# Narrow attentions: projections spread over the loop's first steps, the selection split in halves, the pair mask added in sixteen 32x32 pieces

## The reference

```
q = norm(x) Wq + bq;  k = ctx Wk + bk;  v = ctx Wv + bv
scores[h] = q[h] k[h]^T / sqrt(8)      (+ mask: layer 0 by key, layer 2 by query and key)
out[h]    = softmax(scores[h]) v[h]
layer 2:  of the 128 queries of each head only the 27 with the largest |q[h]|^2 keep their out[h]
x = x + tanh(g) * (out Wo + bo)
```

## Time and profile before

| | us |
|---|---|
| median of 3 runs | 1951.07 (1949.83 to 1951.59) |
| the profiled execution, its own time | 1948.23 |
| its span from the first instruction to the last | 1946.2 |
| TensorE busy | 1779.9 (91% of the span) |
| VectorE busy | 1115.4 (57%) |
| ScalarE busy | 861.5 (44%) |
| GpSimd busy | 613.5 (32%) |

### The profile page before, as it was taken

How to read it: one execution, slowest core, us unless ns; L and a number is a source line. 1 busy time by engine, 2 the same in 40 slices (tenths; PEclk the granted TensorE clock), 3 DMA queues, 4 the chain that set the end, 5 groups by cost and what they waited for, 6 DMA issues and landing times. The chain is left out here.

```text
span 1946.2 us, 43912 instructions
## 1 busy us (share of the span) xinstructions
PE 1779.9 (91%) x16273; PEld 1149.1 (59%) x16273; DVE 1115.4 (57%) x2416; ACT 861.5 (44%) x2151; POOL 613.5 (32%) x1047
## 2 busy tenths in 40 slices
PE   5999878999999999769889999979999989997797
PEld 3555453778778778557763444436777754554343
DVE  4677667566666665561554555552222246776886
ACT  4455425455555555425452333334333344543232
POOL 2667318222222222200103544400000006763440
PEclk9999969999999999869998999978999998999898
DMA  4000040000000000101010000000000010000001
GB/s 108 2 3 3 27 118 6 6 5 7 7 4 7 7 7 2 44 0 44 1 45 1 2 2 2 2 1 0 1 0 0 0 44 2 3 3 2 0 0 43
DMA packets 47708, 27.17 MB, mean 14 GB/s; under 512 B 10928, under 2 KB 44592, under 8 KB 47536
## 3 DMA queue, kind: packets, MB, share of 16 engines
q1 hardware_dynamic: 42800, 24.64, 4.5%
q10 hardware_dynamic: 4736, 0.15, 0.1%
HBM read 22.69 MB, written 2.10 MB: 13 GB/s over the span
## 5 line engine op out<-in xcount | busy, mean ns | idle before, releaser
L708 DVE TENSOR_REDUCE neg_max<-scores 128x8 f32<-128x1024 f32 x192 | 234.8, 1225 | 162.4 <-PE scores L523 66.8
L1708 POOL TENSOR_TENSOR probs<-probs,inverse 128x512 f32<-128x512 f32 x128 | 133.3, 1041 | 337.6 <-DVE inverse L1908 337.6
L651 ACT ACTIVATE probs<-turned 128x1024 f32<-128x1024 f32 x128 | 131.1, 1024 | 224.0 <-PE turned L538 224.0
L493 PE MATMUL scores<-k_diag,q_all 32*128 32x512 f32 x768 | 221.9, 663 | 2.2 <-DVEq L701 2.2
L510 PE MATMUL turned<-q_diag,k_all 32*128 32x512 f32 x768 | 222.0, 653 | 1.1 <-ACT probs L651 1.1
L389 POOL TENSOR_TENSOR k_diag<-k_all,hmask 128x512 f32<-128x512 f32 x96 | 99.8, 1041 | 328.0 <-ACT k_all L630 292.1
L1842 ACT ACTIVATE probs<-scores,neg_max 128x128 f32<-128x128 f32 x512 | 180.7, 387 | 5.3 <-DVE neg_max L1900 5.3
L1409 ACT ACTIVATE hidden_f<-hb_f,b_f 128x512 f32<-128x512 f32 x128 | 88.0, 687 | 130.1 <-PE hb_f L1356 129.9
L1365 PEld LDWEIGHTS yb_f<-w_f,hidden_f 128*128 128x128 f32 x1024 | 119.2, 192 | 14.8 <-issue 14.8
L1365 PE MATMUL yb_f<-w_f,hidden_f 128*128 128x128 f32 x1024 | 119.3, 275 | 0.0
L1356 PE MATMUL hb_f<-xn_all_f,w_f 128*128 (+1 forms) x256 | 118.1, 605 | 0.0
(11 more groups left out here) (292 smaller groups left out, 3675.4 us busy)
## 6 DMA issues: line engine op xcount, KB each, us to landing
ctx_t<-in_ctx_t_dram SPq DMA_DIRECT2D x24, 256.0 KB, 3.2
w_f<-in_L_ffn_W_dram SPq DMA_DIRECT2D x16, 256.0 KB, 3.1
x_state<-in_x_dram SPq DMA_DIRECT2D x4, 512.0 KB, 8.4
ctx_t<-in_ctx_t_dram SPq DMA_DIRECT2D x16, 128.0 KB, 2.1
out_dram<-x_state SPq DMA_DIRECT2D x4, 512.0 KB, 5.4
w_f<-in_L_ffn_We_dram SPq DMA_DIRECT2D x1, 1024.0 KB, 6.8
taps_f<-in_L_ffn_conv_w_dram SPq DMA_DIRECT2D x1, 768.0 KB, 6.4
w_e_f<-_ffn_expert_weights_dram SPq DMA_DIRECT2D x1, 512.0 KB, 4.4
```

The source lines that it names most:

```text
L493: last = nc.tensor.matmul(scores[pair][:, (g % 2) * 512:(g % 2 + 1) * 512], cols(q_all, b, S)[quad_rows(g), :], k_diag[quad_rows(g), b % 2 ...
L651: nc.scalar.activation(probs[:, b % 2, pair, :], turned[:, :], ACT.Exp, **bias).then_inc(s["exp_done"], 1)
L708: v.tensor_reduce(neg_max[:, b % 2, 8 * pair:8 * pair + 8], scores[pair][:, :].rearrange("p (h k) -> p h k", k=S), axis=X_AXIS, op=ALU.max ...
L1708: nc.gpsimd.tensor_tensor(p4, p4, inverse[:, n % 2, CH * h:CH * h + CH].unsqueeze(2).to_broadcast([P, CH, S]), ALU.mult).then_inc(s["prob_ ...
```

## The change

Three things change in the same function.

- **Projections.** `keys_values` is split into `keys` and `values`. Layers 0 and 3 make only two chunks of keys and values and one of queries ahead of the loop (KV0 = 2, TQ0 = 1), layer 2 four chunks of keys and values and all of the queries. The others are made in the loop's first steps: `first_fills` (turned x, keys) at a step's start into `scores[1]`, `second_fills` (queries, values) before `contexts` into `scores[0]`. TensorE waits for the maximum that was last taken from these banks, and each `direct` waits until ScalarE has read the fills. ScalarE reads the first kind before its exponents of the step and the second kind after them. VectorE normalises chunk b+5 within the step in layers 0 and 3; in layer 2 VectorE also copies the turned x, which ScalarE did.
- **Selection.** It gets tiles of its own and works on halves of 16 sequences. The first half is chosen before VectorE's first `maximum`, its ties in the steps -2 and -1; the second half's rounds stand in the steps 1 to 4 and 6, its ties in the steps 8 and 9.
- **Pair mask.** The mask comes laid out by the host in four rotated copies, the last two transposed (128x512 in place of 128x128), and is added by `masks` in 32x32 pieces of the array: eight products of 512 columns for the direct scores and eight for the turned ones, each with another pair of row group and column group.

```diff
-    LATE = 0 if select else 2
+    KV0, TQ0 = (4, NG) if select else (EARLY, 1)
...
-        k_ps, v_ps = turned[:, 0:GW], turned[:, GW:2 * GW]
-        q_ps = [scores[1][:, 0:GW], scores[1][:, GW:2 * GW]]
-        xt_ps = [scores[0][:, 0:GW], heads[1][:, :]]
+        lower, upper = slice(0, GW), slice(GW, 2 * GW)
+
+        def kv_bank(c):
+            if c >= KV0:
+                return scores[1][:, upper], scores[0][:, upper]
+            return (turned[:, lower], turned[:, upper]) if c % 2 == 0 else (heads[0][:, :], heads[1][:, :])
+
+        def tq_bank(c):
+            half = upper if c < TQ0 and c % 2 else lower
+            return scores[1][:, half], scores[0][:, half]
...
+        def first_fills(b):
+
+            return [("t", c) for c in [b + 4] if TQ0 <= c < NG] + [("k", c) for c in [b + 3 + KV0] if KV0 <= c < NG]
+
+        def second_fills(b):
+            return [("q", c) for c in [b + 4] if TQ0 <= c < NG] + [("v", c) for c in [b + 3 + KV0] if KV0 <= c < NG]
...
+            for c in range(EARLY):
+                keys(c)
+                values(c)
+            turn_queries(0)
+            for c in range(TQ0):
...
-            for c in range(EARLY, NG - LATE):
-                keys_values(c)
-            pe.wait_ge(s["q_ready"], NG)
-            pe.wait_ge(s["xnt_done"], NG)
-            if select:
-                topk["tensor"](pe)
+            for c in range(EARLY, KV0):
+                pe.wait_ge(s["k_ready"], c - 1)
+                if c % 2:
+                    topk["norms_read"](pe)
+                keys(c)
+                pe.wait_ge(s["v_ready"], c - 1)
+                values(c)
...
                 if pair == 0:
                     pe.wait_ge(s["kdiag_ready"], b + 1)
+                    pe.wait_ge(s["q_ready"], max(min(b + 1, NG), TQ0))
+                    pe.wait_ge(s["v_ready"], min(b + KV0, NG))
+                    if select:
+                        topk["ranks_read"](pe, b - AHEAD)
+                else:
+                    pe.wait_ge(s["xnt_done"], max(min(b + 2, NG), TQ0))
+                    pe.wait_ge(s["k_ready"], min(b + 1 + KV0, NG))
+                    if select:
+                        topk["ties_read"](pe, b - AHEAD)
...
+            def masks(b_direct, pair, b_cross):
+
+                sides = [(scores[pair], 0, b_direct)] * real(b_direct) + [(turned, 2, b_cross)] * real(b_cross)
+                if mask == "keys" and real(b_direct):
+                    for g in (2 * pair, 2 * pair + 1):
+                        last = nc.tensor.matmul(scores[pair][:, (g % 2) * 512:(g % 2 + 1) * 512], one_row[quad_rows(g), b_direct, :],
                                                 key_rows[quad_rows(g), :].unsqueeze(1).to_broadcast([32, 4, S]),
                                                 start=False, stop=True)
-                    else:
-                        last = nc.tensor.matmul(out, st.identb[:, :], pair_bias[:, :].unsqueeze(1).to_broadcast([P, 4, S]),
-                                                start=False, stop=True)
-                last.then_inc(s_done[pair], 1)
-
-            def crosswise_shift(b, pair):
+                    last.then_inc(s_done[pair], 1)
+                if mask == "pairs":
+                    for out, first, b in sides:
+                        for half in range(2):
+                            for r in range(4):
+                                c = (r + first + half) % 4
+                                last = nc.tensor.matmul(out[quad_rows(c), half * 512:(half + 1) * 512],
+                                                        st.identb[quad_rows(r), quad_rows(r)],
+                                                        pair_bias[quad_rows(r), first + half, :].unsqueeze(1).to_broadcast([32, 4, S]),
+                                                        start=False, stop=first == 0, skip_group_check=True)
+                        if first == 0:
+                            last.then_inc(s_done[pair], 1)
...
-                if mask == "pairs":
-                    for g in (2 * pair, 2 * pair + 1):
-                        nc.tensor.matmul(turned[:, (g % 2) * 512:(g % 2 + 1) * 512], st.identb[:, :],
-                                         pair_turned[:, :].unsqueeze(1).to_broadcast([P, 4, S]), start=False, stop=False)
...
             for b in range(-AHEAD, NB + 1):
+                todo = first_fills(b)
+                if todo or select and b in topk["turn_at"]:
+                    wait(pe, s["max1_done"], b + AHEAD)
+                for kind, c in todo:
+                    fill[kind](c)
+                if select:
+                    topk["turn"](pe, b)
                 direct(b + AHEAD, 0)
                 crosswise(b, 1)
-                direct_mask(b + AHEAD, 0)
-                crosswise_shift(b, 1)
+                masks(b + AHEAD, 0, b)
+                shifts(b, 1)
                 sums(b - 1)
-                if -2 - LATE < b <= -2:
-                    keys_values(NG + b + 1)
                 turn_shift(b + 2)
                 direct(b + AHEAD, 1)
                 crosswise(b + 1, 0)
-                direct_mask(b + AHEAD, 1)
-                crosswise_shift(b + 1, 0)
+                masks(b + AHEAD, 1, b + 1)
+                shifts(b + 1, 0)
+                todo = second_fills(b)
+                if todo or select and b in topk["turn_at"]:
+                    wait(pe, s["max0_done"], b + AHEAD + 1)
+                for kind, c in todo:
+                    fill[kind](c)
+                if select:
+                    topk["rank"](pe, b)
...
             for b in range(-AHEAD, NB):
+                for kind, c in first_fills(b):
+                    read[kind](c)
...
+            normalise(0)
+            dve.wait_ge(loaded, n_loaded)
+            v.tensor_scalar(scaled_bq[:, :], b_q[:, :], scale, None, ALU.mult).then_inc(s["bq_ready"], 1)
             if select:
-                topk["vector"](dve, link)
+                topk["start"](dve)
+            normalise(1)
+            v.tensor_scalar(b_o[:, :], b_o[:, :], gate, None, ALU.mult).then_inc(s["bias_ready"], 1)
             if mask == "keys":
                 dve.wait_ge(s["mask_in"], 80)
-                link(v.tensor_scalar(key_rows[:, :], key_int[:, :], 0, -BIG, ALU.is_equal, ALU.mult))
                 link(v.tensor_scalar(key_cols[:, :], key_int_t[:, :], 0, -BIG, ALU.is_equal, ALU.mult))
-                dve.sem_inc(s["ready"], 1)
-            elif mask == "pairs":
-                dve.wait_ge(s["pair_done"], 1)
-                link(v.tensor_copy(pair_turned[:, :], shift_ps[0][:, 0:S]))
-                dve.sem_inc(s["ready"], 1)
+                v.tensor_scalar(key_rows[:, :], key_int[:, :], 0, -BIG, ALU.is_equal, ALU.mult).then_inc(s["mask_ready"], 1)
+            if select:
+                choose_first, choose_start, choose_middle = topk["vector"](dve)
+                for c in range(NG):
+                    copy_turned(c)
+                    if c + 2 < NG:
+                        normalise(c + 2)
+            if mask == "pairs":
+                dve.wait_ge(s["mask_in"], 16)
+                v.tensor_copy(pair_bias[:, :, :], pair_f[:, :, :]).then_inc(s["mask_ready"], 1)
+            if select:
+                choose_first()
...
+        def ahead_of_loop():
+            read_norms(0)
+            next_eight(0, 0)
+            read_norms(1)
+            for k in range(1, rounds + 1):
+                next_eight(0, k)
+            limits(0)
+
+        def step_start(b):
+            if b in turn_at:
+                ties(turn_at[b])
+            if b - 1 in turn_at:
+                ranks(turn_at[b - 1])
+
+        def step_middle(b):
+            if 1 <= b <= rounds + 1:
+                next_eight(1, b - 1)
+            if b == rounds + 3:
+                limits(1)
...
+    if name == "mask_1x1xSxS2_ff0":
+        a = np.concatenate([np.roll(a if i < 2 else a.T, -32 * i, axis=0) for i in range(4)], axis=1)
```

More of the change, by code:

```diff
@@ L452, in keys_values @@
                                             start=True, stop=True)
                 last.then_inc(s["v_done"], 1)
[L455 to L465 removed]
+            fill = {"t": turn_queries, "q": queries, "k": keys, "v": values}
@@ L510, in crosswise @@
                     nc.tensor.matmul(turned[:, (g % 2) * 512:(g % 2 + 1) * 512], cols(k_all, b, S)[quad_rows(g), :],
-                                     q_diag[quad_rows(g), b % 2, :, :].rearrange("p h k -> p (h k)"), start=True, stop=False)
-            def direct_mask(b, pair):
-                if not real(b) or mask is None:
-                    return
-                for g in (2 * pair, 2 * pair + 1):
-                    out = scores[pair][:, (g % 2) * 512:(g % 2 + 1) * 512]
-                    if mask == "keys":
-                        last = nc.tensor.matmul(out, one_row[quad_rows(g), b, :],
+                                     q_diag[quad_rows(g), b % 2, :, :].rearrange("p h k -> p (h k)"), start=True, stop=False,
@@ L663, in _ @@
```

(34 more changed lines are left out.)

184 lines of the change are left out of this document (86 added, 98 removed).

## The result

| | before | after |
|---|---|---|
| median, us | 1950.45 (1948.91 to 1951.59, 4 runs) | 1889.46 (1887.46 to 1891.34, 4 runs) |
| profiled execution, own time | 1948.23 | 1887.46 |

What follows compares the result with a forecast made beforehand. TensorE was taken to bound the kernel. Layer 2's loop at -28.3 us and the three starts at -22.1 sum to -50.4, giving 1897.8 or 1900.7, so 1900 us; own range 1887 to 1908, wider 1885 to 1932.

Steps and rivals of the forecast that it cites:

- What bounds: Layer 2's loop: TensorE is busy for 160.00 of 160 us, so its work sets the 7.55 us step.
- The mask group: Layer 2's half-steps: sixteen pieces run in one pass, 0.45 us for 0.96, saving 28.6 us over 56 half-steps.
- The rival of banks that queue: Mask pieces: row groups writing one PSUM bank queue, so sixteen take 3.6 us and the kernel 2094; chance 6%.
- The rival of one axis at a time: Mask pieces sharing a row or column group don't run at once: four passes, nothing saved, 1932 us; chance 10%.
- The selection: Layer 2: the half ahead of the loop is covered; the second half's rounds fit VectorE's free time in the steps.
- The ties: Layer 2's loop: added small products and a wait of direct for the ranks lose 1.0 us, 0 to 3.
- a sign of being wrong: Layer 2's loop: steps 1 to 9 longer than the later ones by more than 0.5 us each.
- The start of layer 2: Moved projections fill waits and keep the clock up, with start masks and ties cheaper: 11.2 us won.
- remnants: Loop starts: TensorE waits and shape changes left by the fills, 2.6 us in layers 0 and 3, 2.0 in layer 2.
- The start of layer 3: Fills win idle time and half clock: 3.1 + 8.7 - 2.6, less 0.9, so 8.3 us.
- The idle term: Layer 3's start: 3.1 us of TensorE idle time to be won, against 2.6 us of new waits.
- The start of layer 0: Fills win idle time and half clock: 3.6 + 1.6 - 2.6, so 2.6 us.

Runs made afterwards that it cites:

- the kernel with four uses of each place: The changed kernel with the same sixteen 32x32 products placed on only the four diagonal array pieces, each used four times; 1927.18 us, ratio 0.9886 to before.
- the two edits that bring waits back: Against the changed kernel, all keys and values of layer 2 ahead of its loop, 1896.95 us; or the second half's selection rounds ahead, 1893.57 us.
- The two edits of layers 0 and 3: Against the changed kernel, both layers' keys and values ahead of their loops, 1899.00 us; or all their projections ahead, 1907.07 us.
- whole masks: The changed kernel with the mask added by four whole 128x128 products again, all else kept; 1924.62 us, ratio 0.9872 to before.
- the pieces alone: The kernel before with only the mask laid out in rotated copies and added in sixteen 32x32 pieces; 1915.85 us, ratio 0.981.
- keys and values ahead in layers 0 and 3: The changed kernel with all keys and values of layers 0 and 3 made ahead of the loop; 1899.00 us, ratio 0.9745 to before.

## Why the prediction was right, and where its sizes were off

**What bounds.** Right. TensorE fills layer 2's loop before and after, and the step fell by twice what the mask group did (1.18 of 1.21). No other engine became the bound: VectorE is busy for 89.26 of 140 us there.

**The mask group.** The mechanism was right and the size off: "one pass and 15 x 0.01 ... 0.45 us" measured 0.37. Of the term's parts, the 0.22 of one pass holds (0.97 - 0.55 = 0.42 for two more uses of each place); what is left, 0.37 - 0.22 = 0.15, is change of shape and starts together, for which 0.23 stood. How it divides between the two stays open. Over 56 half-steps the saving is 0.59 x 56 = 33.0 us, not 28.6. By the Trainium skill's TensorE: Matmul & The Clock Gate, Part 3, with its 4 ns for each further piece, the estimate was 0.44. That figure runs from the first start to the last end, and so read the trace agrees: the second row of eight ends at 1037.42 + 0.41 = 1037.83, 0.44 after 1037.39, with an end that the profile models. What the step pays is the distance to the next group's start, 0.37, since the shift starts before that end.

**The rival of banks that queue** has fallen. The four row groups of each group of pieces write one bank, in different partitions, and the sixteen still take 0.37 us, a tenth of the 3.6 of that rival. Even if the four banks were served side by side, one row group at a time in each, four passes of 0.22 would be needed, 0.88. The Trainium skill's TensorEngine Tiling (Array Packing), Gotcha 1, says that different row tiles cannot use one PSUM bank at the same time; read as a whole bank, it isn't borne out here. Nothing here was run with two row groups on the same partitions of a bank. The rival of one axis at a time has fallen as well: by it the sixteen would take 0.96, and only the kernel with four uses of each place does.

**The selection.** Right. The half ahead of the loop is covered: VectorE was ready 0.62 us before TensorE's scores were. The prediction's 2.5 us free for VectorE in a step of 6.5 is 2.2 by its own row (6.5 - 90.60/160 x 7.55), still room for a round. The ties cost the loop two longer steps, 7.20 and 6.66 us against 6.34, so 1.2 us, for which 1.0 stood. Only the first of them passes the 0.5 us that the prediction gave as a sign of being wrong if each step showed it. What the split of the selection is worth for its first half wasn't run by itself, with the projections moved and the whole selection ahead. For the whole rest of the stage after its start the forecast was -28.3, and -33.8 was measured; 4.4 of the 5.5 between them are the mask group's.

**The start of layer 2.** From the stage's first mark to the first `direct` of b = 1 it took 1054.56 - 985.17 = 69.4 us before and takes 1036.32 - 979.50 = 56.8 now: 12.6 saved, for which 11.2 stood. (The 2.0 us of remnants in that sum is 2.3 by its own parts for four steps.) Pieces of 0.37 instead of 0.45 explain 0.3 of the difference. The clock no longer falls behind the start's waits, and each of the two edits that bring waits back lengthens the time at 1.2 GHz too (24 and 12 us for 9). How much of the 4 to 8 us of those edits is the wait and how much the clock isn't separated.

**The start of layer 3** was mis-sized: 8.3 us stood, 5.1 were measured (6.2 from the first turned x on, and 1.1 lost ahead of it). The same 440 products, from the first turned x to the `contexts` of b = 3, before and after:

```profile
1579.23:1637.74 58.51, 55.40 (x440) 29.54 (x438) 27.09 (x48) 30.68 (x44) 21.71 (x43) 0.85 0.06 17
1524.92:1577.20 52.28, 50.06 (x440) 26.01 (x438) 28.67 (x48) 31.36 (x44) 22.62 (x43) 1.00 0.06 17
```

The idle term held: 3.1 less 2.6 of remnants left 0.5 us, and idle time fell by 0.9, with waits of 0.74, 0.39 and 0.81 us in the place of 0.32, 0.74 and 2.06. The clock rose to full as forecast, but the term for it, 8.7 - 0.9 = 7.8 us, is the one that failed: TensorE's busy time fell by 5.3. A half-step with `sums` takes 4.13 us at 1.2 GHz in the trace of before (1621.31 to 1625.44) and 2.30 at the full clock (1628.49 to 1630.79). By that, an estimate, the 16.1 us that TensorE was busy at 1.2 GHz there were worth 7.1; by the rest, 1.8 us, the same products take longer in their new order. Which of them do, and why, wasn't shown. The 1.1 us ahead were put at nothing: from the stage's mark on, TensorE ran at 1.2 GHz for 9 us, 7 before, which covers them if all of the work followed the clock.

**The start of layer 0** is as forecast (-2.5 for -2.6), in part because two sizes offset each other: TensorE's waits fell by 1.8 us (3.5 to 1.7) where 1.0 was expected (3.6 - 2.6), and its time at 1.2 GHz fell from 3.4 to 1.1 us, worth at most 1.2 where 1.6 stood. The two edits of layers 0 and 3 show that the fills hold 9.8 to 12.5 us in both layers together, more than the change won over the kernel before, so their comparison isn't the change undone: the order of the work ahead of the loop also differs.

**The stages that the change doesn't touch** were taken as equal, and gave 6.8 us: half of the 14 us by which their time at 1.2 GHz fell (161 to 147). Over all kernels here their sum lies between 1192.5 and 1199.2, for the same work. The largest part, 3.4 us, is in the stage behind layer 2's attention; it is also there with whole masks (278.3) and half there with the pieces alone (280.0, 281.7 before). With keys and values ahead in layers 0 and 3 the stage takes 279.7, though it and layer 2 are as after. The time at 1.2 GHz in it was 31 us before, 25 after. What decides when the clock falls there is open.

In sum, of the 10.4 us that the forecast missed in the span, the untouched stages hold 6.8, layer 2 6.9, and layer 3 -3.2.

## What to carry to other kernels

Products on 32 rows and 32 columns that each have their own row group and column group can run as one pass, also where they share PSUM banks in different partitions; count how often the busiest place is used, not the instructions. A wait of 2 us on the engine that bounds is worth more than its own length when a stretch at half clock follows (behind waits of 2.0 to 3.4 us it was 3.4 to 31 us long here): look in the profile at the granted clock behind each such wait, and move independent work into it. A piece of work can be split by when its parts are needed: here the half ahead of the first result was covered, the rounds in the loop cost nothing, and the ties cost 1.2 us.

## What was not expected of the hardware

- Sixteen products in sixteen places take 0.37 us to the next group's start, change of tile shape included, where four whole products take 0.96.
- The stretch at 1.2 GHz behind much the same wait of TensorE for the selection was 13.6 us long in one kernel (2.23 us of wait) and 31 us in another (2.0 us); behind a longer wait, of 3.40 us for the first maximum, it was 3.4 us. With the pieces alone, one of four runs was 11 us shorter than the other three, which lie within 0.5 us; its mean granted clock was higher, 0.946, and no trace shows where.
- Stages with the same instructions differ by up to 6.8 us in their sum between kernels that differ only elsewhere, with the time that they run at 1.2 GHz.
